# Graph network on one Trainium2 core: when the scratch matrix is zeroed, and in which order ScalarE copies the node tiles

## The reference

```python
h = (feat - mean) * rsqrt(var + EPS) * gamma + beta      # over nodes
feat_in  = h @ W_in  + b_in
feat_out = h @ W_out + b_out
a_in  = segment_sum(feat_in[src]  * iw[:, None], dst)
a_out = segment_sum(feat_out[dst] * ow[:, None], src)
xi = concatenate((a_in, a_out), 1) @ W_x2i + b_x2i
hh = h @ W_h2h                                           # h again: needed turned
h = new_gate + input_gate * (h - new_gate)               # gates from xi + hh
```

## Time and profile before

| | us |
|---|---|
| median of 3 runs | 3275.62 |
| lowest, highest | 3275.25, 3277.7 |
| the profiled execution | 3277.98 |
| its span, first to last instruction | 3276.2 |
| last zeroing DMA landed | 352.75 |
| one-hot tiles | 435.8 to 1241.2 |

### The profile page before, as it was taken

How to read it: one execution, slowest core, us unless ns; L and a number is a source line. 1 busy time by engine, 2 the same in 40 slices (tenths; PEclk the granted TensorE clock), 3 DMA queues, 4 the chain that set the end, 5 groups by cost and what they waited for, 6 DMA issues and landing times.

```text
span 3276.2 us, 37001 instructions
## 1 busy us (share of the span) xinstructions
PE 2563.7 (78%) x14593; PEld 1400.9 (43%) x14593; DVE 1677.4 (51%) x1848; ACT 1262.3 (39%) x2535; POOL 801.4 (24%) x611
## 2 busy tenths in 40 slices
PE   0551057777777777888888889998999999999896
PEld 0320023333333333444444434555565664555543
DVE  3441679999999995554555545112012324132313
ACT  0137057777777504666666523101001111121203
POOL 3000467777777731222222200000000000000000
PEclk9885579999999999999999999999999999999897
DMA  9999843333333317889888652644434326454362
GB/s 373 404 387 409 255 92 58 58 58 58 58 57 54 33 13 187 214 212 228 216 215 215 168 131 47 135 92 90 99 81 101 83 71 128 103 122 100 79 145 66
DMA packets 326008, 466.24 MB, mean 142 GB/s; under 512 B 106089, under 2 KB 261992, under 8 KB 325604
## 3 DMA queue, kind: packets, MB, share of 16 engines
q1 hardware_dynamic: 246445, 420.30, 47.5%
q0 software_dynamic: 57360, 0.92, 4.8%
q10 hardware_dynamic: 22023, 42.59, 4.0%
HBM read 313.97 MB, written 149.75 MB: 142 GB/s over the span
## 4 chain that ended last, share of the span: by engine, by line
PE 42%; DMA 19%; POOL 11%; SPq 11%; DVE 8%; issue 6%; ACT 3%; DVEq 0%; ACTq 0%; POOLq 0%
PE psum L1046 24%; POOL cell_mat L511 11%; PE psum L994 11%; DMA cell_mat<-ROW 10%; SPq L344 10%; DMA Q<-cell_mat 8%; PE psum L926 3%; DVE AR L1330 3%; DVE Q L1395 2%; ACT Q L660 2%; PE psum L1063 1%; DMA cell_mat<-SA 1%; PE psum L1073 1%; DVE ROW L1389 1%; ACT Q L651 1%
## 5 line engine op out<-in xcount | busy, mean ns | idle before, releaser
L1046 PE MATMUL psum<-FR 125*128 125x500 f16 (+1 forms) x4200 | 823.2, 355 | 20.8 <-DVE FR L1449 20.8
L511 POOL DMA_INDIRECT cell_mat<-ROW x391 | 618.8, 1582 | 538.4 <-DMA cell_mat<-SA 324.0
L896 PE MATMUL psum<-AR,Q 128*128 128x500 f16 (+1 forms) x2737 | 593.3, 356 | 183.8 <-DVE AR L1330 180.0
L1330 DVE TENSOR_SCALAR AR<-Q,ROW 128x3125 f16<-128x3125 f16 x391 | 721.4, 1901 | 7.5 <-PE psum L896 0.9
L1046 PEld LDWEIGHTS psum<-FR 125*128 125x128 f16 x4200 | 387.6, 98 | 429.9 <-issue 45.3
L896 PEld LDWEIGHTS psum<-AR,Q 128*128 128x128 f16 x2737 | 237.3, 98 | 455.8 <-DVE AR L1330 182.4
L1476 DVE SCALAR_TENSOR_TENSOR Q<-psum,small,ROW 128x1000 f32<-128x1000 f32 (+1 forms) x42 | 48.2, 1147 | 713.4 <-PE psum L1046 713.4
L1395 DVE SCALAR_TENSOR_TENSOR Q<-Q,small 125x1000 f16<-125x1000 f32 (+1 forms) x175 | 248.9, 1426 | 267.4 <-ACT Q L660 267.2
L660 ACT ACTIVATE Q<-Q,small 125x1000 f16<-125x1000 f32 (+1 forms) x175 | 262.3, 1499 | 121.5 <-DMA Q<-cell_mat 121.0
L940 PE MATMUL psum<-Q,FR 125*128 125x500 f16 (+1 forms) x1050 | 240.8, 368 | 73.1 <-DVE Q L1395 71.2
L994 PE MATMUL psum<-wl,Q 128*125 128x256 f32 (+1 forms) x1100 | 286.8, 401 | 5.7 <-ACT Q L717 3.0
(11 more groups left out here) (271 smaller groups left out, 2331.6 us busy)
## 6 DMA issues: line engine op xcount, KB each, us to landing
cell_mat<-SA SPq DMA_DIRECT2D x39, 3000.0 KB, 31.6
Q<-cell_mat SPq DMA_DIRECT2D x150, 703.1 KB
FR<-count_mat SPq DMA_DIRECT2D x180, 585.9 KB
AR<-cell_rows ACTq DMA_DIRECT2D x47, 640.0 KB, 4.1
count_mat<-Q SPq DMA_DIRECT2D x150, 117.2 KB
AR<-in_edge_attr SPq DMA_DIRECT2D x13, 960.0 KB, 4.8
Q<-in_edge_attr SPq DMA_DIRECT2D x48, 256.0 KB, 4.2
cell_mat<-ROW POOLq DMA_INDIRECT x391, 3.1
```

What stands on the lines that cost most here:

```text
L511: pool.indirect_dma_start(out=cell_mat, out_offset=bass.IndirectOffsetOnAxis(ap=at[c % VALS][:, k:k + 1], axis=0), in_=vals[c % VALS][:, k ...
L896: last = pe.matmul(a, own_attr, onehot[t % 3][:, t0:t0 + nt], start=t == 0, stop=t == ET - 1, skip_group_check=True)
L1046: last = pe.matmul(a[:, hh, 0:w], parts[:, c, t, f], slot(m, j)[:, i_, :], start=t == 0 and c == 0, stop=t == NT - 1 and c == 1, skip_grou ...
L1330: dve.tensor_scalar(onehot[t % 3], iota16, dst_c[:, t:t + 1], None, ALU.is_equal).then_inc(S["onehot_ready"], 1)
```

## The change

Two things are changed.

1. SyncE waits, before the first zeroing DMA, until both loads of x (`x_in`) and all twelve loads of raw weights (`raw_in`) have landed.
2. In the feature stage ScalarE copies the turned tile t+1 before the projected tile t. The slots `hT` are eight instead of four, and stand in `FR` at columns 10440 to 12439. This lies inside `feat[1]`, so ScalarE waits for all stores of slots before it writes the first part of `feat[1]`.

```diff
-        hT = lambda t: Q[:, XW + (t % 4) * 2 * P:XW + (t % 4 + 1) * 2 * P].rearrange("p (h n) -> p h n", h=2)
+        hT = lambda t: FR[:, 10440 + (t % 8) * 2 * P:10440 + (t % 8 + 1) * 2 * P].rearrange("p (h n) -> p h n", h=2)
...
-        hT_out = [sem(f"hT_out{s}") for s in range(4)]
+        hT_out = [sem(f"hT_out{s}") for s in range(8)]
...
             sp.wait_ge(S["zeros"], 1)
+            sp.wait_ge(S["x_in"], 32)
+            sp.wait_ge(S["raw_in"], 16 * 4 * LAYERS)
             flat = cell_mat.rearrange("a b -> (a b)")
             for j in range(3 * CELLS // SLAB):
...
-            for s in range(4):
-                sp.wait_ge(hT_out[s], 16 * len(range(s, NT, 4)))
+            for s in range(8):
+                sp.wait_ge(hT_out[s], 16 * len(range(s, NT, 8)))
...
-                act.dma_start(hT_d[:, :, t * P:(t + 1) * P].rearrange("h p n -> p h n"), hT(t)).then_inc(hT_out[t % 4], 16)
-            for t in range(NT):
-                act.wait_ge(S["tr_done"], TR_AT["feat", t])
-                if t >= 4:
-                    act.wait_ge(hT_out[t % 4], 16 * (t // 4))
-                act.activation(hT(t), trp[:, t % 2, 0:2 * P].rearrange("p (h n) -> p h n", h=2), ACT.Copy).then_inc(S["tr_read"], 1)
+                act.dma_start(hT_d[:, :, t * P:(t + 1) * P].rearrange("h p n -> p h n"), hT(t)).then_inc(hT_out[t % 8], 16)
+            for t in range(NT + 1):
+                if t < NT:
+                    act.wait_ge(S["tr_done"], TR_AT["feat", t])
+                    if t >= 8:
+                        act.wait_ge(hT_out[t % 8], 16 * (t // 8))
+                    act.activation(hT(t), trp[:, t % 2, 0:2 * P].rearrange("p (h n) -> p h n", h=2), ACT.Copy).then_inc(S["tr_read"], 1)
                 if t:
-                    keep(t - 1)
-                act.wait_ge(S["out_done"], OUT_AT["feat", t])
-                act.activation(Bn[0][:, t], outp(t)[:, 0:D], ACT.Copy).then_inc(S["nat_ready"], 1)
-                act.activation(Bn[1][:, t], outp(t)[:, D:2 * D], ACT.Copy).then_inc(S["out_read"], 1)
-            keep(NT - 1)
+                    u = t - 1
+                    keep(u)
+                    act.wait_ge(S["out_done"], OUT_AT["feat", u])
+                    act.activation(Bn[0][:, u], outp(u)[:, 0:D], ACT.Copy).then_inc(S["nat_ready"], 1)
+                    act.activation(Bn[1][:, u], outp(u)[:, D:2 * D], ACT.Copy).then_inc(S["out_read"], 1)
...
+                if n == PIECES:
+                    for s in range(8):
+                        act.wait_ge(hT_out[s], 16 * len(range(s, NT, 8)))
```

## The result

The changed kernel takes 3287.0 us (median of 10 runs, 3284.76 to 3292.52) against 3277.8 us for the kernel before, run beside it (median of 10, 3275.09 to 3281.45). The ratio is 1.0031 with a 95% interval of 1.0022 to 1.0041: slower by 0.31%, about 9 to 10 us. The profiled execution has a span of 3283.3 us, 7.1 us more than before.

What follows compares the result with a forecast made beforehand. The prologue's zeroing bytes were taken to bound the kernel through the last zero's landing. Terms 9.3 (later zeroing) + 0 (feature stage) + 0 (store density) gave 3287.3 us on the profiled execution, 3284.9 on the median; range 3275.5 to 3291.

Steps and rivals of the forecast that it cites:

- What bounds: First 460 us: the last zero's landing at 352.75 us sets the end one to one; earlier VectorE arrival is worth nothing.
- Start of the zeroing: Prologue: zeroing held until x and raw land starts near 33 us, 3.7 MB left unmoved, last zero 9.3 us later.
- The 2 us between the issue and the first packets: Prologue, after raw lands: wait, issue and first packet of the zeroing estimated at 2 us, half covered by ScalarE-queue weight loads.
- Rival B: x and raw loads: each packet costs the same whatever its size; plus 12.7 to 17 us, 3288.3 to 3292.6; chance 0.16.
- Rival A: x and raw loads without zeros: still 350 GB/s or more, deficit 1.4 us, end at 3277.0 us; chance 0.22.
- The mechanism: DMA engines in the prologue: 1 KB packets mixed with 4000-byte zeroing packets ride nearly free, 46 against 72 ns each.
- Feature stage: ScalarE's new copy order: 2.4 us a tile, 20 us off an 86 us stage starting about 40 us earlier; worth 0.
- the 60 us: Feature stage: the total gain of some 60 us, which only lengthens VectorE's 39 us wait to about 100 us.
- VectorE's air: Before the peak search: VectorE's idle wait for the first peak load, 39 us before the change, about 100 us forecast after.
- Density of the stores: Zeroing beside the hT stores: 4.6 us lost at 386 against 408 GB/s; change taken as 0, 1 us kept for range.
- rival C: Zeroing during the feature stage: the stores win back up to 4.6 us, so not slower, 3272.4 us; chance 0.10.
- the forecast's own case: End of the kernel: slower by 6 to 12 us, given a chance of 0.52.

## Why the prediction was right, point by point

*What bounds.* Right. The end hangs on the landing of the last zero (one more zeroing DMA: 7.5 us later there, 0.22% or 4 to 10 us at the end) and not on VectorE's arrival (order and slots alone: 0.9996).

*Start of the zeroing.* Right in sign and size, 9.3 us forecast for the landing and 11.1 measured; at the end 9.2 us between the medians. The first zero was to be issued at about 31 us and came at 34.4. But the sum came out so near by terms that were off in opposite directions, and that was luck. I priced x and raw at one rate, 207 GB/s. x went at 177 to 187 GB/s and with a tail of 86 (the run that waits for x alone issues its first zero at 27.8 us, where 1.49 MB at 207 GB/s give 21.2), raw at 265 to 289 (6.6 us more instead of 9.5). The 2 us between the issue and the first packets weren't lost either: from 34.4 to 35.4 us the engines already move 373 GB/s. The expectation of the run that waits for x only was built on the same error and failed openly. Rival B, one price for each packet, is refuted: 35 ns for raw's packets against 95 for x's. Rival A, the price of the mix alone too, is wrong for x by half, and for raw it is nearer, 265 to 294 GB/s against its 350. By the packet rule of the Trainium skill ("DMA: Bandwidth & Descriptors", section "Why small descriptors are slow (HBM only)"), a fixed cost for each packet, raw with its 256-byte rows would be the dearer of the two for a byte. The traces show the opposite, 177 to 187 GB/s for x and 265 to 294 for raw, so the rule does not account for what is slow here.

*The mechanism.* That zeros beside x make it nearly free was an inference from 46 ns against 72 ns a packet. Three zeroing DMAs ahead of the wait show it: 47 ns instead of 95, from 199 to 386 GB/s, and the end back at 1.0003. That it is the length of the zeros' packets that does it stays an inference.

*Feature stage.* Worth 0, as forecast, and VectorE arrives 59 us earlier (256.9 instead of 315.7), as the 60 us said. The two parts of that were off: the stage begins 44 us earlier, not 40, and gets 15 us of the 20 back. The first tiles are better than said (2.16 us, not 2.4), the last eight worse (about 3), because the stores back up. I had taken their 7.9 us to landing from the slower pace of the kernel before, and left out that a store's issue can hold ScalarE. The stores' line, to hold against the earlier trace rows, and one copy from ScalarE's list:

```profile
DMA to landing us min/median/max: 7.5/19.3/22.2
...
184.29 1.36 ACT L581 ACTIVATE FR<-AR,small 125x1280 f16<-125x1280 f32 x1 [2.82 <-DMA hT_d<-FR]
```

At the denser pace the stores fall behind: those issued up to 120 us land in 7.5 to 14.8 us, the ten from 133.7 us on in 21.4 to 22.2. No wait of ScalarE for a slot shows, so eight just hold, but the issue of each of these ten takes 2.6 to 3.7 us. The new wait ahead of the second half of the split cost 2.8 us where I had given it nothing. VectorE's air swallowed it.

*Density of the stores (rival C).* Nothing: 352.8 against 353.0 us for the last zero.

*Chances.* The outcome, 9.2 us, lies in the forecast's own case (6 to 12). Of the 10 us at the one-hot tiles the profiled execution shows 7 at its end; the stage that loads the cells (first to last load) took 648.1 us before and 645.2 after. It took 648.0 with the wait alone, 644.8 with the order alone, 642.9 with one more zero, 641.3 with the wait for x only and 647.2 with three zeros first. It follows neither the wait nor the order, so I take it for a variation between executions.

## What to carry to other kernels

When a long bulk transfer bounds a stage, holding it back "to let the small loads pass" costs the bytes that the small loads leave unmoved: in x's time 161 GB/s were moved instead of 393, in the raw weights' time some 280 instead of 405. A few of the long transfers issued first can fill that time; three of them brought the loss here from 11.1 to 4.2 us at the last zero, and more wasn't tried. And before an early stage is sped up, see what its successor waits for. Here an earlier feature stage was worth nothing, and moving the peak loads out from behind the zeroing came with 22 to 24 us at the end in the best kernels, with VectorE 6.5 us earlier than before as well as with VectorE 58 us earlier.

## What the runs showed of the hardware that I had not expected

- At a DMA share of 1.11 to 1.15 the engines moved between 86 GB/s (23 to 27 us) and 289 (30 to 34.4 us), and at 1.03 they moved 400. The share says that packets are in flight, not that bytes move; GB/s has to be read beside it.
- Without zeros beside them, x's rows (1 KB, 25 for each partition) went at 163 to 195 GB/s and took 95 ns a packet, raw's rows (1 KB and 256 bytes) at 265 to 294 GB/s and 35 ns.
- A load of five partitions, 125 packets, issued last, had a tail of 79 GB/s from 24 to 26 us; issued first it had none. The last zero landed 1.6 us earlier by that, in one profile.
- Stores of 125 KB beside the saturated zeroing landed in 7.6 to 8.8 us at one each 3.2 us. At one each 2.16 us they fell behind, to 22.2 us, and then ScalarE needed 2.6 to 3.7 us to issue each, instead of 0.37.
